# Two layers of cross attention on one core: x loaded turned, first output product kept turned, all engine orders rewritten

## The reference

```python
# layer 0, for s in (a: keys ctx_512, v: keys fside)
q = ln(x) @ Wq_s + bq_s; k = ln(c_s) @ Wk_s + bk_s; v = ln(c_s) @ Wv_s + bv_s
out_s = softmax(q @ k.T * E**-0.5) @ v @ Wo_s + bo_s
res = out_a + out_v + x
x1 = ln(res) @ fc_W + fc_b + res
# layer 1, keys ctx_512, not normalised
Q = x1 @ Wq + bq; K = ctx @ Wk + bk; V = ctx @ Wv + bv
out = x1 + softmax(Q @ K.T * H**-0.5) @ V @ Wo + bo
```

## Time and profile before

| | us |
|---|---|
| runs | 169.98, 168.39, 169.56 |
| median of the runs | 169.56 |
| span of the profiled execution, first to last instruction | 167.2 |
| PE busy in that span | 155.5 (93%) |
| PE weight loads busy | 121.7 (73%) |
| DVE busy | 131.4 (79%) |
| ACT busy | 124.2 (74%) |
| POOL busy | 76.4 (46%) |

### The profile page before, as it was taken

The page is one execution under the profiler, slowest core; times in us unless marked ns, Lnnn a source line. Parts: engine busy times, 40 slices in busy tenths (PEclk is TensorE's granted clock), DMA queues, the critical chain, the costliest instruction groups (busy, mean ns, idle before and its releaser), DMA issues.

```text
span 167.2 us, 6323 instructions
## 1 busy us (share of the span) xinstructions
PE 155.5 (93%) x2442; PEld 121.7 (73%) x2442; DVE 131.4 (79%) x400; ACT 124.2 (74%) x384; POOL 76.4 (46%) x104
## 2 busy tenths in 40 slices
PE   6799998999999999799999999989999999999682
PEld 6769674896689687767786787667788887995350
DVE  1693499999899789999999996497688997596531
ACT  3431559869988979599879788977978789866930
POOL 2026269789676523714979624194532022110210
PEclk9965579999999999999999999999999999999955
DMA  5999999900001010101010011001010100101113
GB/s 139 299 380 380 378 379 378 364 33 0 2 4 67 0 67 0 68 2 67 4 63 4 0 67 65 6 0 67 0 67 20 47 6 4 67 0 65 63 67 125
DMA packets 9982, 15.93 MB, mean 95 GB/s; under 512 B 1249, under 2 KB 3682, under 8 KB 9954
## 3 DMA queue, kind: packets, MB, share of 16 engines
q1 hardware_dynamic: 9522, 15.14, 25.1%
q10 hardware_dynamic: 432, 0.40, 1.0%
HBM read 11.35 MB, written 4.19 MB: 93 GB/s over the span
## 4 chain that ended last, share of the span: by engine, by line
PE 73%; DVE 9%; ACT 7%; issue 4%; DMA 3%; POOL 2%; ACTq 1%; POOLq 0%
PE ps L1526 9%; PE ps L1465 8%; PE ps L1508 7%; PE ps L1576 5%; PE ps L1516 5%; PE ps L1496 4%; PE ps L1541 4%; PE ps L1534 4%; PE ps L1485 4%; PE ps L1456 4%; PE ps L1475 4%; PE ps L1449 4%; DMA cf_sb<-in_cf 3%; PE ps L1568 3%; ACT exp L632 3%
## 5 line engine op out<-in xcount | busy, mean ns | idle before, releaser
L384 POOL TENSOR_TENSOR prob<-exp,rsum 128x512 f32<-128x512 f32 x16 | 16.7, 1042 | 23.5 <-DVE rsum L1025 23.5
L390 POOL TENSOR_TENSOR prob<-exp,rsum 128x256 f32<-128x256 f32 x16 | 9.8, 613 | 29.0 <-DVE rsum L1085 29.0
L356 POOL TENSOR_TENSOR z_sb<-x_sb,x_rstd 128x512 f32<-128x512 f32 x15 | 15.4, 1040 | 15.9 <-ACT x_rstd L543 14.1
L632 ACT ACTIVATE exp<-ps,exp_bias 128x64 f32<-128x64 f32 x64 | 19.2, 315 | 3.5 <-DVE exp_bias L1080 3.4
L1061 DVE SCALAR_TENSOR_TENSOR x_sb<-ps,res_rstd,res_sb 128x128 f32<-128x128 f32 x64 | 19.2, 342 | 0.2 <-issue 0.2
L1465 PE MATMUL ps<-zT_sb,m 128*128 128x512 f32 x32 | 17.8, 645 | 0.0
L1526 PE MATMUL ps<-wd,resT_sb 128*128 128x130 f32 x128 | 17.6, 280 | 0.0
L1508 PE MATMUL ps<-w,mix_sb 128*128 128x128 f32 x128 | 17.5, 280 | 0.0
L378 POOL TENSOR_TENSOR cfn_sb<-cf_scaled,cf_shift 128x512 f32<-128x512 f32 x15 | 15.6, 1042 | 4.0 <-issue 2.9
L1526 PEld LDWEIGHTS ps<-wd,resT_sb 128*128 128x128 f32 x128 | 15.6, 191 | 2.0 <-ACT resT_sb L609 1.5
L371 POOL TENSOR_TENSOR cf_scaled<-cf_sb,cf_rstd 128x512 f32<-128x512 f32 x15 | 15.4, 1043 | 2.7 <-ACT cf_rstd L555 2.5
(11 more groups left out here) (141 smaller groups left out, 384.2 us busy)
## 6 DMA issues: line engine op xcount, KB each, us to landing
x_sb<-in_x SPq DMA_DIRECT2D x16, 256.0 KB, 6.8
out<-out_sb SPq DMA_DIRECT2D x16, 256.0 KB, 2.0
cf_sb<-in_cf SPq DMA_DIRECT2D x15, 256.0 KB, 7.1
ct_sb<-in_ct SPq DMA_DIRECT2D x16, 128.0 KB, 7.9
w_sb<-in_w SPq DMA_DIRECT2D x1, 448.0 KB, 5.6
cf_sb<-in_cf ACTq DMA_DIRECT2D x1, 256.0 KB, 4.9
...
```

What stands on the lines that cost most here:

```text
L356: pool.tensor_tensor(z_sb[:, g % Z_SLOTS, :, :], x_sb[:, g, :, :], wide_x(g), ALU.mult).then_inc(z_pool, 1)
L384: pool.tensor_tensor(prob0[:, g % PROB0_SLOTS, :, :, :], exp0[:, g % EXP0_SLOTS, :, :, :], wide0(rsum0, g), ALU.mult).then_inc(prob0_pool, 1)
L632: last = nc.scalar.activation(exp1[:, g % EXP1_SLOTS, p, :], ps[:, bank + u, v * S:(v + 1) * S], ACT.Exp, bias=exp1_bias[:, g, p:p + 1], a ...
```

## The change

- **x turned.** Groups 0 to 3 (`TURNED`) still go through `z`, `zT` and `copy_zT`. From group 4 on x is loaded a second time, already turned (`xt_sb`). What it is multiplied by lies along the free dimension then, so the reciprocal roots of two groups (`rows`, which also hold the keys' scale and shift) are turned by one PE transpose (`turn_rows`), copied by ACT (`copy_rowsT`), stored to DRAM (`store_rows`), read back with a broadcast over 128 partitions (`spread_x`, 128x1024), and POOL multiplies (`scale_xt`) straight into `zT_sb`.
- **First output product and dense kept turned.** `out0` is one product of 512 columns with `w01` stationary, so that its result has features on the partitions; its bias is now a column (`out0_bias`) added in `residual`, which reads `xt_sb` and writes `resT_sb`. `dense` takes `resT_sb` without a transpose or copy before it. `resN` turns it back (4 transposes) only for the statistics, which DVE reads in PSUM. ACT multiplies dense's result (`gain`, 4 instructions of 128x128; DVE's `early_gain` for groups 14 and 15), `x1T` turns that, and `x1` is one DVE instruction of 128x512 that adds residual and bias and leaves `x1T_sb`.
- **Softmax 1's maximum** and its correction are kept in PSUM, in columns behind the scores.
- **Fewer constants in the ramp.** The value bias goes through `bv_full` and `out0_bias`, not through the mix weights; the load of `rows_sb` and its four matmul passes (L1410) are gone, and the ones for `ln1_b` ride along as column 129 of `affine_a1` and `affine_v1` (written by POOL, `tails`). Keys are shifted for the scores only; `mix0` reads the scaled ones.
- **Slots.** `x_sb` has 4, `xt_sb` 8, `cf_sb` 9 and `ct_sb` 6 slots in place of 16, so the loads on SP wait for `x_stats_done`, `res_done`, `mix1_made` and `s1_made`, and the stores stand among them.
- **All orders are new.**

```diff
-X_BATCHES = [[0], [1], [2, 3], [4, 5], [6, 7], [8, 9], [10, 11], [12, 13], [14, 15]]
+TURNED = [0, 1, 2, 3]
+BATCHES = [[0], [1], [2, 3], [4, 5], [6, 7], [8, 9], [10, 11], [12, 13], [14, 15]]
+SPREAD_FROM = 3
+KEY_BATCHES = []
+Z_ON_DVE = []
+CF_ON_DVE = []
+GAIN_ON_DVE = [14, 15]
+PROB1_ON_DVE = [15]
...
+            def load_x(g):
+                need(sp, x_stats_done, g - X_SLOTS + 1)
+                if g >= X_SLOTS and g - X_SLOTS in TURNED:
+                    z_ready(sp, g - X_SLOTS)
+                sp.dma_start(x_sb[:, g % X_SLOTS, :, :], x[g, :, :, :]).then_inc(x_in[g % X_SLOTS], 16)
+            def store_rows(b):
+                at = b - SPREAD_FROM
+                sp.wait_ge(rowsT_copied, at + 1)
+                sp.dma_start(rows_dram[at, :, :], rowsT[:, at % SPREAD_SLOTS, :]).then_inc(rows_stored[at % SPREAD_SLOTS], 16)
+            def spread_x(b):
+                at = b - SPREAD_FROM
+                sp.wait_ge(rows_stored[at % SPREAD_SLOTS], 16 * (at // SPREAD_SLOTS + 1))
+                if at >= SPREAD_SLOTS:
+                    sp.wait_ge(zT_scaled, BATCHES[b - SPREAD_SLOTS][-1] + 1 - len(TURNED))
+                sp.dma_start(x_spread[:, at % SPREAD_SLOTS, :, :].rearrange("p g t -> p (g t)"),
+                             rows_dram[at, 0:8, :].rearrange("r t -> (r t)").unsqueeze(0).broadcast_to([D, 8 * P])
+                             ).then_inc(x_spread_in[at % SPREAD_SLOTS], 16)
+            def turn_rows(b, bank, *reads):
+                pe.wait_ge(x_rstd_done, b + 1)
+                pe.wait_ge(cf_shift_done, b + 1)
+                after(*reads)
+                nc.tensor.transpose(ps[0:40, bank, 0:P], rows[:, b, :], ident[:, :]).then_inc(rowsT_made, 1)
+            def scale_xt(g):
+                slot, half = spread_at(g)
+                slot_in(pool, xt_in, g, XT_SLOTS)
+                spread_in(pool, x_spread_in, g)
+                need(pool, t0_made, g - ZT_SLOTS + 1)
+                pool.tensor_tensor(zT_sb[:, g % ZT_SLOTS, :], xt_sb[:, g % XT_SLOTS, :], x_spread[:, slot, half, :],
+                                   ALU.mult).then_inc(zT_scaled, 1)
+            def gain(g, bank):
+                act.wait_ge(dense_made, g + 1)
+                act.wait_ge(res_rstd_done, g + 1)
+                need(act, x1T_made, g - GAIN_SLOTS + 1)
+                for p in range(PAIRS):
+                    at = (p % 2) * (D + 2)
+                    last = nc.scalar.mul(gain_sb[:, g % GAIN_SLOTS, p, :], ps[:, bank + p // 2, at:at + D],
+                                         res_rstd[:, g, p // 2, p % 2:p % 2 + 1])
+                last.then_inc(gain_act, 1)
 def residual(g, bank):
...
-                v.tensor_tensor(res_sb[:, g % RES_SLOTS, :, :], by_pair(ps[:, bank, :]), x_sb[:, g, :, :], ALU.add
-                                ).then_inc(res_done, 1)
+                v.scalar_tensor_tensor(resT_sb[:, g % REST_SLOTS, :], ps[:, bank, :], out0_bias[:, 0:1],
+                                       xt_sb[:, g % XT_SLOTS, :], ALU.add, ALU.add).then_inc(res_done, 1)
...
 def x1(g, bank):
...
-                for p in range(PAIRS):
-                    last = v.scalar_tensor_tensor(x1_sb[:, g % X1_SLOTS, p, :], duos[:, p // 2, p % 2, 0:D],
-                                                  res_rstd[:, g, p // 2, p % 2:p % 2 + 1],
-                                                  res_sb[:, g % RES_SLOTS, p, :], ALU.mult, ALU.add)
+                v.scalar_tensor_tensor(x1T_sb[:, g % X1T_SLOTS, :], ps[:, bank, :], row_bias[:, 0:1],
+                                       resT_sb[:, g % REST_SLOTS, :], ALU.add, ALU.add).then_inc(x1T_done, 1)
...
 def out0(g, bank, *reads):
...
-                for u in range(DUOS):
-                    for v in range(2):
-                        p = 2 * u + v
-                        last = mm(ps[:, bank, p * P:(p + 1) * P], mix0_sb[:, g % MIX0_SLOTS, u, v, :, :], w01[:, 0:D],
-                                  start=True, stop=True)
+                mm(ps[:, bank, :], w01[:, 0:D], mix0_sb[:, g % MIX0_SLOTS, :, :, :, :], start=True, stop=True
+                   ).then_inc(out0_made, 1)
```

More of the change, by code:

```diff
@@ L204, in col64 @@
             return tile[0:C, at:at + 1]
-        def row(name):
-            return rows_sb[0:1, ROWS.index(name), :]
         def by_pair(ps):
@@ new lines, in _ @@
+            bias_scores1(3, 4)
+            diff_scores0(7, 0)
+            key_biases(4, 6)
+            stats_res(5, 2)
+            x1(4, 1)
+            recip_sum1(3)
+            stats_cf(11)
+            max_scores0(8, 4)
+            diff_scores0(8, 4)
+            sum_exp0(7)
+            final(2, 0)
+            max_scores1(4, 4)
+            recip_sum0(7)
+            top_scores1(4, 4)
+            bias_scores1(4, 4)
+            residual(6, 2)
+            key_biases(5, 6)
+            recip_sum1(4)
@@ new lines, in _ @@
+            final(5, 3)
+            max_scores0(11, 1)
+            diff_scores0(11, 1)
+            stats_res(9, 0)
+            stats_cf(15)
+            recip_sum1(7)
+            final(6, 6)
+            sum_exp0(11)
+            recip_sum0(11)
+            max_scores0(12, 2)
+            max_scores1(8, 4)
+            top_scores1(8, 4)
+            diff_scores0(12, 2)
+            residual(10, 1)
+            bias_scores1(8, 4)
+            sum_exp0(12)
+            stats_res(10, 0)
+            recip_sum0(12)
@@ L1870 @@
              np.pad(np.stack([take(n) for n in COLS64], axis=1), ((0, P - C), (0, 0)))], axis=1)),
-        "rows": np.ascontiguousarray(np.stack([take(n) for n in ROWS])[None]),
     }
```

2007 lines of the change are left out of this document (1069 added, 938 removed).

## The result

The changed kernel takes **156.38 us** (median of 4 runs, 155.49 to 158.29), the kernel before, on the same chip in turn, 168.97 us (4 runs, 168.25 to 169.98). The ratio is 0.925, with a 95% interval of 0.916 to 0.933: 12.6 us or 7.5% less. 159.6 us was forecast. The profiled execution has a span of 154.9 us where the kernel before had 167.2, so 12.3 us less.

What follows compares the result with a forecast made beforehand. PE was taken as first, with 73% of the chain and parts of the path on DVE. Terms -3.8 - 0.5 - 0.7 - 2.5 - 2.5 = -10.0 us took 167.2 to 157.2, plus 2.4 gave 159.6 us; range 152 to 166.5.

Steps and rivals of the forecast that it cites:

- x turned, -3.8: Groups 4 to 15: PE transposes of x gone, 4.5 us less, row transposes 0.7 us more; net -3.8 us.
- `out0`, -0.5: First output product: one 512-column product takes 0.86 us in place of 0.89 for four, 16 x 0.03 = -0.5 us.
- Dense kept turned, -0.7 on ACT and -2.5 on DVE: Dense part: ACT copies go, `gain` comes, `x1` becomes one DVE instruction; path shorter by 0.7 us (ACT) and 2.5 (DVE).
- The maximum in PSUM, 0: Softmax 1's small DVE operations: 5.7 us either way on DVE, a third at most on the path; taken as 0.
- The ramp, -2.5: Folding before the first `t0`: passes with `rows_sb` gone, some folds moved later; -2.5 us, from +1 to -6.
- near 12: Sign in the changed profile's ramp: the first `t0` near 12 us in place of 16.7.
- DVE is the bound: Rival, 20 to 100 us: PE's gain falls beside DVE, only DVE's 4.8 us is felt; 164.8 us, chance 0.17.
- The engines free each other: Rival: the chain outside PE shrinks by a sixth, 7.5 us, and the ramp gives 4.5; 153.3 us, chance 0.19.
- Weight loads count: Rival, `out0`: every weight load stands alone, so 11.6 us go in place of 0.5; 148.5 us, chance 0.03.
- The SP queue: Rival, SP's in-order transfers: loads behind `store_rows` and `spread_x` come late; 177.6 us at 3 us late each, chance 0.07.

Runs made afterwards that it cites:

- the five and the eight starts of the first `out0`: Profiled starts: kernel before and four variants not touching the ramp, 30.54 to 35.05 us; changed kernel twice and six variants, 28.08 to 29.30 us.
- the pair of parts tried together: Kernel before with only the last of four `z` transposes in groups 4 to 15 and `x1` as one plain sum: 168.44 us, ratio 0.996.
- `out0` in four: Changed kernel with `out0` as four products of 128 columns again: 157.76 us, ratio 0.933, middle 0.2 us longer.
- the four undone parts: Changed kernel with, one at a time, x's transposes on PE, `out0` in four, `x1` in four, maximum in SBUF: 161.57, 157.76, 161.25, 161.89 us.

## Why the prediction was right, and where its terms were off

The forecast was 159.6 us with a range of 152 to 166.5, and 156.4 was measured. The direction, and the reading that PE comes first with parts of the path on VectorE, held: PE's busy time fell, DVE came to 121.4 where 123 was foreseen, ACT to 114.1 for 113. The sum was 3 us short. Its terms:

- *x turned, -3.8.* The transposes were taken at 4.5 of their 5.3 us, with 0.7 against it for the turned rows. Undoing them in the changed kernel costs 4.0 us in the middle, so the size is about right there. But 36 of the 48 (4.0 us), taken alone out of the kernel before, gave 0.5. The term holds only with the rest.
- *`out0`, -0.5.* 0.2 in the middle. The broadcast and store traffic, whose cover I named as what could fail, cost at most 1.9 us of waits, and none that moved the end can be seen. `scale_xt` was not the same product as `z`, as I had put it: 1274 ns for 1040. POOL has the room.
- *Dense kept turned, -0.7 on ACT and -2.5 on DVE.* `x1` at 742 ns was foreseen as 730. `gain` at 374 ns lay near the far end of its bounds (248 to 385), with 16.0 us for the 15 taken, because its source in PSUM didn't make it short. Undoing `x1` cost 2.6 us of the middle and 3.2 to 4.7 of the time. The term stands in size, again only with the rest: alone in the kernel before, `x1` gave 0.4. ACT's 0.7 was not tested by itself.
- *The maximum in PSUM, 0.* **This is the step that failed.** I had bounded it by 5.7 us of busy time either way, "and a third of it at most on the path", and took the middle. It is worth 3.3 us of the middle alone, of 4.2 us of busy time, and 4.8 when undone, of 5.7: some 80% of its busy time is on the path. I had read the mean of 358 ns as the sum's own cost. It is a mixture: 161 ns at the median, and up to 905 ns where the sum waits for GpSimd. The same trace shows the wait a second time, in the row of `bkq`: an operation on one column with both inputs in SBUF took 994 ns and ended 15 ns after a GpSimd instruction. So engines don't meet at semaphores alone, as I had written at the start. The Trainium skill has a page that I had set beside these means afterwards (VectorE: DVE Perf Modes, the section on the TRN2 errata): operations whose source is SBUF pay a fixed extra latency per instruction, and its table has the larger fixed part for VectorE's PSUM sources. The runs show no difference of either kind between the two places: while GpSimd isn't running, a sum of four columns takes 141 to 165 ns with both inputs in SBUF and 141 to 171 ns with one in PSUM.
- *The ramp, -2.5.* It gave 3.75 in the two profiles (4.1 between the means of the five and the eight starts of the first `out0` listed above). The first `t0` came at 14.4 us, 2.3 us earlier, which is what the term gives; the "near 12" among my signs doesn't follow from it. `fold_am`, moved up to the front, left PE idle for 0.75 us until `w_sb` had landed, a wait which my part on the ramp doesn't have. The rest of the gain came behind it: the clock rose by 20 us, as forecast, and `zT`, `cfT` and the folds of 18 to 24 us ran at 2.4 GHz.
- *Not in the sum:* 1.6 us of the tail. Among single profiles of the kernel before and its variants the tail varies from 20.3 to 22.0 us, so at least part of it is chance.

The middle's terms were 3.8 + 0.5 + 0.7 + 2.5 = 7.5 us less and 6.9 were measured, although the maximum, put at 0, gives 3.3 alone. So the sum came out near because the other terms were too large as terms, by about what the maximum was too small: that part of the hit was luck. A right total does not show right terms.

**The rivals.** *DVE is the bound* fell: 164.8 us was its time, VectorE holds 1% of the chain, and taking 4 us of it away changes nothing. *The engines free each other* looks nearest in the chain, though the pair of parts tried together in the kernel before shows little of it (1.4 us of the middle for 0.5 + 0.4). The chain outside PE shrank from 45 to 19 us, by more than half and not by a sixth, but PE's own part grew by 14, so that the time stayed above its 153.3. *Weight loads count* fell with `out0` in four. *The SP queue* was not met. A broadcast landed after 4.2 us at the median (3.7 to 6.9), within the 2 to 7 foreseen, and the waits for it come to 1.9 us.

**What paces both kernels.** Work taken from a single engine gives almost nothing, in the kernel before (4.0 us of PE: 0.5; 4.9 of DVE: 0.4; both: 1.4) and in the changed one (4.0 of PE: none; 4.0 of DVE: none). Work added to the changed kernel costs half of itself or more (5.3 of PE: 4.0; 5.1 of DVE: 2.6; 5.7 of DVE in the two small sums: 4.8). Only VectorE's waits for GpSimd, in the row of steps between scores and exps, gave time by themselves when they went (3.3). I read it so: the orders of all engines are written out by hand, each engine waits in order, and they fit durations of their time. With less work at one place, an engine arrives early and waits for the next one in the round; with more, everybody waits for it. The 2.2 us of the middle that neither the maximum (3.3) nor the pair of parts tried together (1.4) explains, and the fact that undoing shows far more than adding, would then be the new orders' share. That share is argued and not shown: for the maximum a part of it is plain, as 12 sums are held up by GpSimd in the new orders and 8 in the old ones. Beyond that, no kernel with all of the old work in new orders, or of the new work in old ones, was run, since the orders name operations that only one of the two has; the four undone parts put back one piece of it each.
